# The steps' places made a row by products with the identity, not by a DMA of single words, and half of their count an iteration later

## What is computed

```python
x = x + gnn(layernorm(x), edge_index, ...)      # attention over the edges, then a dense FFN
x = x + moe(layernorm(x), ...)                  # top 2 of 8 experts

# in gnn:
h = (xn @ W).reshape(N, HEADS, HEAD_DIM)
e = leaky_relu(a_src[src] + a_dst[dst], 0.2)
emax = segment_max(e, dst); ee = exp(e - emax[dst])
alpha = ee / segment_sum(ee, dst)[dst]
agg = segment_sum(h[src] * alpha, dst)
```

## Time and profile before

| what | us |
|---|---|
| median of 3 runs | 3304.02 |
| lowest and highest | 3302.67, 3306.39 |
| the profiled execution | 3309.24 |
| its span, first to last instruction | 3307.6 |
| TensorE busy | 2076.5 (63%) |
| VectorE busy | 1683.3 (51%) |
| ScalarE busy | 1450.4 (44%) |
| GpSimd busy | 1175.7 (36%) |

### The profile page before, as it was taken

One profiled execution on the slowest core, in us unless ns is written; L12 is line 12 of the kernel. 1 busy time (PEld: TensorE's weight loads), 2 busy tenths in 40 slices (PEclk: granted clock), 3 DMA queues, 4 the chain that ended last, 5 costly groups with the idle time before them and its releaser, 6 DMA issues.

```text
span 3307.6 us, 51219 instructions
## 1 busy us (share of the span) xinstructions
PE 2076.5 (63%) x16490; PEld 1777.0 (54%) x16490; DVE 1683.3 (51%) x5236; ACT 1450.4 (44%) x3212; POOL 1175.7 (36%) x1155
## 2 busy tenths in 40 slices
PE   5334554445544455444554445469899499999999
PEld 4223333334333343333433333358878499999999
DVE  6234554445544455444554445587766445555554
ACT  3313333333333333333333333346665466666665
POOL 2444334433344333443344433301323312222223
PEclk8656666666666666666666666679999799999999
DMA  7633333333333333333333333322222444463533
GB/s 187 174 99 91 96 95 105 112 88 96 95 108 99 98 96 95 109 99 98 94 96 109 99 98 88 95 94 65 91 73 67 136 108 97 77 171 51 146 50 40
DMA packets 268719, 329.50 MB, mean 100 GB/s; under 512 B 118550, under 2 KB 207984, under 8 KB 263716
## 3 DMA queue, kind: packets, MB, share of 16 engines
q0 software_dynamic: 63840, 151.61, 19.3%
q1 hardware_dynamic: 204036, 173.54, 17.5%
q10 hardware_dynamic: 576, 1.09, 0.1%
HBM read 431.90 MB, written 95.53 MB: 159 GB/s over the span
## 4 chain that ended last, share of the span: by engine, by line
PE 41%; another core or an unknown queue 30%; DVE 10%; issue 8%; ACT 7%; DMA 1%; SPq 1%; DVEq 1%; POOL 1%; ACTq 0%; POOLq 0%
PE bank L928 14%; PE bank L1104 7%; PE bank L1105 7%; PE bank L1106 7%; PE bank L917 2%; ACT edge_mem L827 1%; DVE edge_mem L994 1%; ACT layer_hid L1199 1%; DVE seg_max L1031 1%; PE bank L514 1%; ACT layer_mem L1198 1%; DVE win_mem L1020 1%; ACT layer_mem L1207 1%; DVE piece_lo L1100 1%
## 5 line engine op out<-in xcount | busy, mean ns | idle before, releaser
L737 POOL DMA_INDIRECT edge_mem<-node_table,src_col x880 | 836.5, 951 | 1188.9 <-PE bank L928 923.0
L928 PE MATMUL bank<-edge_mem 128*128 128x264 f32 x1760 | 554.5, 488 | 4.6 <-DVE edge_mem L994 3.3
L1104 PE MATMUL bank<-expert_rounded 128*128 128x256 f32 x1792 | 509.0, 284 | 34.9 <-DVE expert_rounded L1100 30.2
L1105 PE MATMUL bank<-expert_rounded 128*128 128x256 f32 x1792 | 508.7, 284 | 0.0
L1106 PE MATMUL bank<-expert_rounded 128*128 128x256 f32 x1792 | 508.5, 284 | 0.0
L1041 DVE TENSOR_TENSOR exponent<-edge_mem,bank 128x128 f32<-128x128 f32 x55 | 15.8, 288 | 928.7 <-remote 926.6
L928 PEld LDWEIGHTS bank<-edge_mem 128*128 128x128 f32 x1760 | 429.6, 249 | 108.2 <-issue 5.0
L917 PE MATMUL bank<-cand,edge_mem 128*128 128x9 bf16 x2640 | 81.2, 169 | 644.0 <-DVE cand L1054 618.0
L843 ACT CAST cand<-bank 128x128 bf16<-128x128 f32 x55 | 14.8, 268 | 1019.2 <-remote 1005.2
L917 PEld LDWEIGHTS bank<-cand,edge_mem 128*128 128x128 bf16 x2640 | 75.4, 104 | 682.6 <-DVE cand L1054 655.6
L1104 PEld LDWEIGHTS bank<-expert_rounded 128*128 128x128 f32 x1792 | 345.7, 193 | 35.1 <-issue 35.1
(11 more groups left out here) (229 smaller groups left out, 3968.0 us busy)
## 6 DMA issues: line engine op xcount, KB each, us to landing
expert_rounded<-split_w SPq DMA_DIRECT2D x224, 1024.0 KB
split_w<-piece_hi SPq DMA_DIRECT2D x72, 256.0 KB
split_w<-piece_lo SPq DMA_DIRECT2D x72, 256.0 KB
piece_full<-in_L_ffn_W SPq DMA_DIRECT2D x64, 256.0 KB
expert_mem<-expert_rows SPq DMA_DIRECT2D x224, 64.0 KB, 2.8
edge_mem<-node_table,src_col POOLq DMA_INDIRECT x880
node_table<-win_mem SPq DMA_DIRECT2D x12, 544.0 KB
xn_in<-turned SPq DMA_DIRECT2D x49, 128.0 KB
```

What stands on the lines that cost most here:

```text
L737: pool.indirect_dma_start(gath[g % NGB][:, t, :], None, node_table, bass.IndirectOffsetOnAxis(ap=src_col[:, k, t % 2:t % 2 + 1], axis=0)). ...
L928: ins = pe.matmul(bank[5 + at % 3][:, 0:AGG], onehot[g % 2][:, 2 * k + j, :], gath[g % NGB][:, 2 * k + j, 0:AGG], start=(j == 0), stop=(j ...
L1104: pe.matmul(out_ap, s_hi, m_lo, start=start, stop=False)
L1105: pe.matmul(out_ap, s_lo, m_hi, start=False, stop=False)
```

## The change

Two things, both in the prep.

The row of windows is no longer made through DRAM. `step_win`, `wk_i`, the store at i = 2 and the load at i = 6 are gone. At i = 4 TensorE waits for `steps_located` 2 and multiplies each column of `wf` (128 partitions x 1, the stationary operand) with the identity: four products, each 128 values on partition 0 of bank 7. At i = 9 VectorE waits for them (`win_spread`) and copies the 440 values from PSUM into `win_row`, turning them into integers.

The count of the steps, four pairs of comparison and sum, was done whole at i = 1. Now two pairs stand at i = 2 and two at i = 3, with the locating steps (`tk_i`, `wf`, `kf`) behind them at i = 3 instead of i = 2. GpSimd's gathers stay at i = 3 and 4.

```diff
--- before.py
+++ after.py
@@ -80,7 +80,6 @@
         step_new = dram("step_new", [NK * P, EB])
         step_last = dram("step_last", [NK * P, EB])
         expert_rows = dram("expert_rows", [E * CAP + SLOT, XROW])
-        step_win = dram("step_win", [NK * P, 1], I32)
         WSZ = KC * HID
         PIECE = 512
         NPIECE = 2 * WSZ // PIECE
@@ -172,7 +171,6 @@
         kf, tf, wf = count[:, 0:NK], count[:, NK:2 * NK], count[:, 2 * NK:3 * NK]
         kcol = sb1("kcol", [P, NK], I32)
         tk_i = sb1("tk_i", [P, NK], I32)
-        wk_i = sb1("wk_i", [P, NK], I32)
         iota_i = part(OT0 + 2 * GT * P - P, P).bitcast(I32)
 
         seg_new = [sb1(f"seg_new{i}", [HEADS * GS, EB]) for i in range(2)]
@@ -303,8 +301,8 @@
         res_consts, res_made, res_kept = sem("res_consts"), sem("res_made"), sem("res_kept")
         xn_loaded, residual_written = [[sem(f"{n}{i}") for i in range(2)] for n in ("xn_loaded", "residual_written")]
 
-        prep_loaded, steps_located, win_stored = sem("prep_loaded"), sem("steps_located"), sem("win_stored")
-        firsts_ready, firsts_spread, counted_steps = sem("firsts_ready"), sem("firsts_spread"), sem("counted_steps")
+        prep_loaded, steps_located, win_spread = sem("prep_loaded"), sem("steps_located"), sem("win_spread")
+        firsts_ready, firsts_spread = sem("firsts_ready"), sem("firsts_spread")
         rows_gathered, new_ready, last_ready = sem("rows_gathered"), sem("new_ready"), sem("last_ready")
         steps_stored = sem("steps_stored")
         cols_turned, cols_copied, src_as_float = sem("cols_turned"), sem("cols_copied"), sem("src_as_float")
@@ -543,19 +541,13 @@
         src_rows = src.rearrange("(b e) -> b e", e=EB)
         COLS = (7, 8, 10)
         GATHER_AT = (3, 4)
+        COUNT_AT = (2, 3)
 
         def prep_sp(i):
             if i == 0:
                 with nc.allow_non_contiguous_dma(reason="one element per edge block"):
                     sp.dma_start(first[0:1, :], dst_rows[:, 0:1].rearrange("b o -> o b")).then_inc(prep_loaded, 16)
-            if i == 2:
-                with nc.allow_non_contiguous_dma(reason="one element per step"):
-                    sp.wait_ge(steps_located, 2)
-                    sp.dma_start(step_win.rearrange("(c p) o -> p (c o)", p=P), wk_i[:, :]).then_inc(win_stored, 16)
             if i == 6:
-                with nc.allow_non_contiguous_dma(reason="one element per step"):
-                    sp.wait_ge(win_stored, 16)
-                    sp.dma_start(win_row[:, :], step_win[0:NSTEP, :].rearrange("k o -> o k")).then_inc(prep_loaded, 16)
                 sp.wait_ge(new_ready, 1)
                 sp.dma_start(step_new.rearrange("(c p) e -> p c e", p=P), rows_n).then_inc(steps_stored, 16)
             if i == 9:
@@ -579,6 +571,11 @@
                 pe.wait_ge(firsts_ready, 1)
                 pe.wait_ge(pool_const, 7)
                 pe.matmul(bank[7][:, 0:NEB], ones[0:1, :], first_w[0:1, :], start=True, stop=True).then_inc(firsts_spread, 1)
+            if i == 4:
+                pe.wait_ge(steps_located, 2)
+                for c in range(NK):
+                    ins = pe.matmul(bank[7][0:1, c * P:(c + 1) * P], wf[:, c:c + 1], ident[:, :], start=True, stop=True)
+                ins.then_inc(win_spread, 1)
             if i in COLS:
                 if i == COLS[2]:
                     pe.wait_ge(last_ready, 1)
@@ -603,32 +600,30 @@
                 t = step(dve.memset(first_w[0:1, 0:1], 0.0))
                 dve.wait_ge(dve_step, t)
                 dve.tensor_tensor(first_w[0:1, :], first_w[0:1, :], iota_b[0:1, 0:NEB], ALU.add).then_inc(firsts_ready, 1)
-            if i == 1:
-                t = step(dve.tensor_copy(kf, kcol[:, :]))
-                dve.wait_ge(dve_step, t)
-                dve.wait_ge(firsts_spread, 1)
-                for c in range(NK):
+            if i in COUNT_AT:
+                if i == COUNT_AT[0]:
+                    t = step(dve.tensor_copy(kf, kcol[:, :]))
+                    dve.wait_ge(dve_step, t)
+                    dve.wait_ge(firsts_spread, 1)
+                half = -(-NK // 2)
+                for c in (range(half), range(half, NK))[COUNT_AT.index(i)]:
                     t = step(dve.tensor_scalar(le, bank[7][:, 0:NEB], kf[:, c:c + 1], None, ALU.is_le))
                     dve.wait_ge(dve_step, t)
-                    ins = dve.tensor_reduce(tf[:, c:c + 1], le, AX.X, ALU.add)
-                    if c < NK - 1:
-                        t = step(ins)
-                        dve.wait_ge(dve_step, t)
-                    else:
-                        ins.then_inc(counted_steps, 1)
-                        dve.wait_ge(counted_steps, 1)
-            if i == 2:
+                    t = step(dve.tensor_reduce(tf[:, c:c + 1], le, AX.X, ALU.add))
+                    dve.wait_ge(dve_step, t)
+            if i == COUNT_AT[1]:
                 t = step(dve.tensor_scalar(tf, tf, -1.0, None, ALU.add))
                 dve.wait_ge(dve_step, t)
                 dve.tensor_copy(tk_i[:, :], tf).then_inc(steps_located, 1)
                 t = step(dve.tensor_tensor(wf, kf, tf, ALU.subtract))
                 dve.wait_ge(dve_step, t)
-                dve.tensor_copy(wk_i[:, :], wf).then_inc(steps_located, 1)
-                t = step(dve.tensor_scalar(kf, wf, float(P), None, ALU.mult))
-                dve.wait_ge(dve_step, t)
+                dve.tensor_scalar(kf, wf, float(P), None, ALU.mult).then_inc(steps_located, 1)
+                dve.wait_ge(steps_located, 2)
             if i == 9:
                 wr = win_row[:, :].rearrange("o (g k) -> o g k", k=GS)
-                dve.wait_ge(prep_loaded, 32)
+                dve.wait_ge(win_spread, 1)
+                t = step(dve.tensor_copy(win_row[:, :], bank[7][0:1, 0:NSTEP]))
+                dve.wait_ge(dve_step, t)
                 t = step(dve.tensor_tensor(win_delta[:, :, 1:GS], wr[:, :, 1:GS], wr[:, :, 0:1].to_broadcast([1, NG, GS - 1]), ALU.subtract))
                 t = step(dve.tensor_copy(win_word[:, :], wr[:, :, 0]))
                 dve.wait_ge(dve_step, t)
```

## The result

| what | before | after |
|---|---|---|
| median, us | 3304.02 | 3290.37 |
| lowest and highest of five runs each | 3302.67, 3312.82 | 3287.80, 3296.75 |
| the profiled execution, us | 3309.24 | 3296.75 |
| its span, us | 3307.6 | 3295.1 |
| the edge stage's first gather, us | 116.33 | 106.62 |

The ratio is 0.9958, with an interval of 0.9946 to 0.9969: the changed kernel is faster by 0.4%, more than the 0.2% that can be told from nothing. The forecast was 3292.7 us, in a range from 3287.5 to 3302.

What follows compares the result with a forecast made beforehand. Waits were taken to bound the node stage, each microsecond saved there counting fully: -5.22 + 3.37 for the count, -0.15 at GpSimd, -10.0 from x waits, +0.7 for the copy, sum -11.3; 3304.02 becomes 3292.7 us, range 3287.5 to 3302.

Steps and rivals of the forecast that it cites:

- What bounds, and the words as suspect: Node stage: waits bound it; storing 512 single words probably opens a slow DMA stretch (35.8 to 43.4 us), losing 6.9 us.
- Rival A: Node stage: the slow stretch belongs to the gathers and the row's transfer is hidden anyway; 3301.5 us, chance 0.12.
- Steps 1 to 5: Node stage to block 6's statistics: moved count, earlier gathers and no slow stretch start these statistics 12.0 us earlier.
- Step 6: VectorE at iteration 6: waiting for all gathered rows costs 0, though it could be 1.1 us; -12.0 holds.
- Step 7: VectorE at iteration 9: copying the row out of PSUM costs 0.7 us on the path, leaving -11.3.
- Step 8: TensorE ahead of block 2's products: the four new products take 0.9 us, covered by idle time.
- Step 9: End of the node stage: from the last column turns on, TensorE runs through and this tail moves as a block.
- B: Node stage: the gathers become the bound, half the gain going there or to SyncE's order; 3298.4 us, chance 0.07.
- C: Edge stage: clock granted one product later in each of 55 groups, costing 22 us; slower, 3314.7 us, chance 0.05.

Runs made afterwards that it cites:

- run 1: Kernel before with only the row made by products, the count left whole at iteration 1: 3304.44 us against 3313.01, ratio 0.9971.
- run 3: Changed kernel plus a store of 512 neighbouring single words that nobody reads, at SyncE's iteration 2: 3310.40 us, ratio to before 0.9991.
- run 7: Changed kernel plus a store of 512 neighbouring single words at SyncE's iteration 5, after the last gather's issue: 3300.89 us (one run).
- run 6: Changed kernel plus a store of 512 single words at iteration 2, 64 bytes from one to the next: 3303.12 us (one run).
- run 2: Kernel before with only the count moved, the row still going through DRAM by single words: 3309.68 us, ratio 0.9989.
- run 8: Changed kernel plus two stores of 512 neighbouring single words, one right behind the other, at iteration 2: 3314.89 us (one run).
- v2: Changed kernel with the row packed in the last iteration and the gathers spread over three iterations: 2349.41 us on the third chip, ratio to before 0.9941.

## Why the prediction was right

The sign, the time and the mechanism held. By its steps:

- **What bounds, and the words as suspect**: shown. The stretch is gone without the words (run 1, and the changed kernel), it comes back with words that nobody reads (run 3), and comes without gathers (run 7). Rival A is out. The rule that spoke against the change, a floor of 10.5 ns a packet in the Trainium skill's "DMA: Bandwidth & Descriptors", section "Bandwidth", was taken to make it 0.34 us. The page's figure is the 0.67 us of one load from GpSimd over its 64 packets; taking it for a store from SyncE and sharing the words out over 16 engines was my own step. The words' own packets fit it, as all of them pass within half a microsecond (from 30.6 to 31.1 us, run 3). The stretch of 7.6 us behind them does not, and the measurement decides: the figure prices a packet, not what the store does to the others. Where the words lie 64 bytes apart or more, nothing comes behind them. The rule on which the prediction leaned beside its rows, that the engines read, modify and write below 512 bytes (the Trainium skill, the same page, "Specifications"), isn't the whole of it either: words 64 bytes apart are as far below 512 and cost nothing that can be seen (run 6). I was right to look at the words, with a reason that was half of it.
- **Steps 1 to 5**: block 1 normalized at 17.84 (forecast 17.3), the first gather at 30.16 (29.6): both 0.6 late, as x of block 1 landed 0.6 us later in this execution. From there the distance to the forecast shrinks on the whole, since GpSimd's queue sets the pace and ran a little faster than before: root of block 4 at 35.17 (34.75), block 4 normalized at 36.26 (35.8), statistics of block 5 at 37.75 (37.1), block 5 normalized at 42.30 (42.1), statistics of block 6 at **43.59** (43.4). -11.8 where -12.0 stood.
- **Step 6**, the term that failed: I took 0 for the wait for the gathered rows, with 1.1 as its bound. It is 1.58 us, and 1.4 of that is loss. I had VectorE arrive 4.5 us after the last gather's issue and priced its landing with the x loads, 5.6 us at most. From the last gather's issue at 40.24 to the end of the wait at 47.20 are 7.0 us. The gathers, the x loads and the stores share the engines at that time, and a gather came last of what VectorE waited for. A landing that had been covered by 14.7 us had no row of its own, and should have been taken at its bound rather than at nothing.
- **Step 7**: 0.60 us for the copy, 0.7 taken. **Step 8**: 1.03 us of products, hidden; 0.9 estimated. The places were 2.5 us old by then, not 1.4.
- **Not in the sum**: the slow product passes got 0.2 us slower at one place and 0.2 faster at another.
- **Step 9** held: -9.55 at iteration 10, -9.7 at the first edge gather.

So the node stage gave 9.7 us where 11.3 were summed, 1.4 of the difference by step 6. The medians of the result above differ by 13.7 us all the same. In the profiled executions the 12.5 us of the span are the node stage's 9.7 and some 3 of the edge stage, which stand between group 4 (-9.8) and its last group (-13.2): one group in the changed profile that takes 36.1 us among others of 37.5, and small differences. I have no run that shows these belong to the change: they may as well be the spread of the edge stage, since the kernel before alone ranges over 10 us. On the third chip medians and node stage agree, 9.6 and 9.5 us (with 116.33 as the stage before, which has no profile on that chip). That the time came out 2.3 us below the forecast is thus partly luck; the node stage was forecast 1.6 us too well, and the rest of the program made up for it. B, gathers as the bound, came true in part, by those 1.4 us, and its sign, the wait at the memset of iteration 6, is there. Of C there is no sign on either chip: the edge stage got no longer.

What of my expectations in the runs fell: the size of run 2, the place of the stretch in run 3, the delay of run 7, the doubling of run 8 and the gain of v2. They have one thing in common: a stretch of slow transfers has no fixed price. It cost here what VectorE waited at its next block, and where a stretch begins and what is asked for meanwhile moved it by several microseconds each time.

## What to carry to other kernels

A DMA that writes single words side by side to DRAM can hold up the other transfers for microseconds, however small it is: here 512 words, 7.6 us. Look for stretches in which the DMA engines are busy and move little, and for what was issued a few microseconds before, whose own packets may look quick; then avoid such a write, or lay its words 64 bytes apart. A small relayout between partitions and a row can be done by products with the identity, where TensorE idles anyway. And where a stage is bound by waits, work that no block needs (here the packing, 5 us) belongs behind the last block: it cost its own time here and, behind TensorE's idle time, up to 1.8 us by its clock too.

## What the runs showed of the hardware that was not expected

**Neighbouring words.** 512 words written side by side leave 23 GB/s to everything else for 7.6 us (28 from 34 to 38 us, run 3); 64 bytes apart it is 342 from 34 to 38 us (run 6). The stretch begins 1.7 us after the words' own packets have passed.

**One program, two times.** The kernel before takes 3304 to 3313 us in the result above and on the first two chips of the experiments, and 2364 on the third; the changed one 3290 and 2355. The changed kernel's node stage takes the same time on both. In the edge stage the groups' first gathers are some 20.2 us apart, instead of 37.5 from the fifth group on. Busy time from 400 to 437 us, first of the kernel before in the profile ahead of the prediction, then of the changed kernel on the third:

```profile
400.00:437.00 37.00, 18.15 (x154) 13.70 (x154) 17.85 (x60) 12.47 (x27) 14.78 (x17) 0.64 0.32 91
```

```profile
400.00:437.00 37.00, 32.00 (x289) 24.13 (x290) 32.62 (x104) 22.87 (x52) 28.15 (x30) 0.72 0.69 198
```

TensorE in order of time in a group of each, the same line of the program (L917 before, L912 changed), in the same two profiles:

```profile
149.67 0.17 PE L917 MATMUL bank<-cand,edge_mem 128*128 128x9 bf16 x1 [2.63 <-issue]
151.07 0.17 PE L917 MATMUL bank<-cand,edge_mem 128*128 128x9 bf16 x1 [1.24 <-issue]
153.87 0.17 PE L917 MATMUL bank<-cand,edge_mem 128*128 128x9 bf16 x1 [2.63 <-issue]
```

```profile
156.82 1.45 PE L912 MATMUL bank<-cand,edge_mem 128*128 128x9 bf16 x48
```

In the profile on the slower chip these products come one at a time, 1.4 or 2.8 us apart and with no releaser, while GpSimd issues gathers (one each 1.25 us up to 196.8 us; at 220.05, with none, 48 of them take 1.45 us); ScalarE and VectorE show waits put down to "remote" there, 118.4 and 109.1 us in 200 (400 to 600 us). On the third chip 48 of them run in 1.45 us beside the same gathers, and there are no such waits. What differs between the chips isn't settled by any run here. It matters to a reader of both: what carries from one chip to the other are the microseconds won in a stage that takes the same time on both, not the ratio. That 0.9958 and 0.9960 agree may well be chance, since 9.7 us of 3304 would be 0.9971.
